# Gate rows spread by TensorE, a transposed first attention output, and high/low sums in place of f32 for one chunk

## What is computed

```python
x = x + 0.5 * _L0_ffn_ref(ln(x))    # MOE0_A: 16 experts 128->256->128, gelu, top 2
x = x + _L0_attn_ref(ln(x))         # ATT0: elu+1 features, sums over the sequence
x = x + 0.5 * _L0_ffn_ref(ln(x))    # MOE0_B
x = x + 0.5 * _L1_ffn_ref(ln(x))    # MOE1_A: 16 experts 128->128, relu, top 2
x = x + _L1_attn_ref(ln(x))         # ATT1: causal linear attention, 16 heads of 8
x = x + 0.5 * _L1_ffn_ref(ln(x))    # MOE1_B
```

## Time and profile before

| | |
|---|---|
| median of 3 runs | 703.26 us (699.38 to 709.02) |
| the profiled execution | 708.19 us, span 706.2 us |
| mean granted TensorE clock | 0.964 |
| TensorE busy | 655.9 us (93%) |
| VectorE, ScalarE, GpSimd busy | 465.5, 432.3, 181.3 us |

### The profile page before, as it was taken

How to read it: one execution, slowest core, us unless ns; L and a number is a source line. 1 busy time by engine, 2 the same in 40 slices (tenths; PEclk the granted TensorE clock), 3 DMA queues, 4 the chain that set the end, 5 groups by cost and what they waited for, 6 DMA issues and landing times.

```text
span 706.2 us, 7645 instructions
## 1 busy us (share of the span) xinstructions
PE 655.9 (93%) x2395; PEld 415.2 (59%) x2395; DVE 465.5 (66%) x1059; ACT 432.3 (61%) x922; POOL 181.3 (26%) x132
## 2 busy tenths in 40 slices
PE   3699998999999999999999999999999989889974
PEld 2456565556656555676576666666566645556552
DVE  5677467643447964737769957858886757386752
ACT  4345456444447554697486478657379524968685
POOL 3120000100002111144042025214014432676565
PEclk9899999999999999999999999989999998989998
DMA  8782621063333107612223222200613000000000
GB/s 244 162 164 67 112 63 38 22 122 65 102 75 60 59 3 132 96 26 65 42 61 62 65 55 60 60 1 11 111 60 61 0 1 0 1 15 1 16 16 15
DMA packets 27026, 42.22 MB, mean 60 GB/s; under 512 B 1689, under 2 KB 8938, under 8 KB 26986
## 3 DMA queue, kind: packets, MB, share of 16 engines
q1 hardware_dynamic: 26986, 41.74, 27.1%
HBM read 40.42 MB, written 1.31 MB: 59 GB/s over the span
## 4 chain that ended last, share of the span: by engine, by line
PE 67%; ACT 12%; DVE 9%; SPq 5%; DMA 4%; issue 2%; POOL 1%; POOLq 0%; ACTq 0%; DVEq 0%
PE py L1122 26%; PE ph L900 7%; PE ph L902 7%; PE ph L901 7%; ACT stage L547 5%; ACT bc L547 4%; DMA bc<-comb_rows 3%; PE ps L1030 2%; SPq L358 2%; DVE stage L756 2%; PE ps L1031 2%; PE ps L1032 2%; SPq L331 1%; PE ps L1004 1%; PE ps L1005 1%
## 5 line engine op out<-in xcount | busy, mean ns | idle before, releaser
L596 ACT ACTIVATE g<-ph,b1col 128x512 f32<-128x512 f32 x256 | 172.7, 695 | 153.3 <-PE ph L902 120.1
L1122 PE MATMUL py<-hw,w2s 128*128 128x512 f32 x512 | 250.0, 612 | 1.9 <-DVE hw L859 1.9
L859 DVE TENSOR_TENSOR hw<-g,bc 128x1024 f32<-128x1024 f32 x128 | 166.8, 1310 | 110.4 <-ACT g L596 93.2
L1122 PEld LDWEIGHTS py<-hw,w2s 128*128 128x128 f32 x512 | 97.2, 194 | 77.7 <-issue 64.4
L900 PE MATMUL ph<-xbh,w1h 128*128 128x512 f32 x256 | 137.4, 537 | 0.0
L388 POOL TENSOR_TENSOR rstd<-vare,mhalf 128x4 f32<-128x4 f32 x24 | 35.4, 1477 | 358.3 <-DVE vare L672 358.1
L547 ACT ACTIVATE stage<-ps,comb 128x128 f32<-128x128 f32 x384 | 106.3, 564 | 10.4 <-PE ps L1032 10.2
L902 PE MATMUL ph<-xbh,w1l 128*128 128x512 f32 x256 | 102.7, 401 | 0.0
L901 PE MATMUL ph<-xbl,w1h 128*128 128x512 f32 x256 | 102.6, 401 | 0.0
L448 POOL TENSOR_TENSOR stage<-stage 128x1024 f32<-128x1024 f32 x24 | 57.4, 2393 | 68.4 <-ACT stage L547 68.4
L900 PEld LDWEIGHTS ph<-xbh,w1h 128*128 128x128 f32 x256 | 49.7, 194 | 30.8 <-issue 22.6
(11 more groups left out here) (199 smaller groups left out, 865.0 us busy)
## 6 DMA issues: line engine op xcount, KB each, us to landing
bc<-comb_rows SPq DMA_DIRECT2D x31, 1024.0 KB, 8.8
stage<-in_L_ffn_W_dram SPq DMA_DIRECT2D x4, 512.0 KB, 6.5
X<-in_L_attn_x_dram SPq DMA_DIRECT2D x4, 256.0 KB, 3.1
bc<-comb_rows SPq DMA_DIRECT2D x4, 256.0 KB, 5.5
out_dram<-X SPq DMA_DIRECT2D x4, 256.0 KB, 2.3
comb_rows<-combT SPq DMA_DIRECT2D x8, 32.0 KB, 5.3
side<-in_L_attn_wq_dram SPq DMA_DIRECT2D x1, 64.0 KB
side<-in_L_attn_wk_dram SPq DMA_DIRECT2D x1, 64.0 KB
```

Of the source, the lines that this page charges most:

```text
L596: nc.scalar.activation(g[:, s % 2, h, 0:w], ph[:, (HC * s + h) % RING_PH, 0:w], ACT.Gelu, bias=b1col[:, HC * e + h:HC * e + h + 1]).then_i ...
L859: V.tensor_tensor(hw[:, s % RING_HW, :, 0:w], g[:, s % 2, :, 0:w], bc[:, s // GQ % 2, s % GQ, 0:w].unsqueeze(1).to_broadcast([P, HC, w]), ...
L1122: ins = T.matmul(py[:, 0:cols], w2s[:, w], hw[:, s2 % RING_HW, h, 0:cols], start=e2 == 0 and h == 0, stop=False)
```

## The change

Five edits and a new `TURNS` table.

1. The gate rows of the first three experts (`PE_GATES = 3`) are no longer read back from DRAM: TensorE spreads each over 128 partitions of `ps` by a matmul of a column of `ident` with `combT`, and VectorE reads them there. The fourth still comes by DMA.
2. ATT0's output is one matmul of `wos` by `vv` (128x512), so that it comes out transposed; the bias is added by the Gelu on ScalarE; four transposes on TensorE bring `osb` back, and VectorE adds from `ps`.
3. W2 and `expert_w` are loaded from ScalarE's DMA queue.
4. `EXACT_CUM` is (3, 4, 5): of the chunks that occur, 2 leaves it and 3 stays, so ATT1 of chunk 2 is summed from `kvh` and `kvl`.
5. The transpose of `expert_b` (start of `wt`) waits for three `hw` as well.

```diff
-    "ACT": ("l2 h l2 h2 l h9 m2 l3 m2 l2 m2 l m2 l3 m4 l2 m4 l m2 l4 m24 l3 m2 h m2 h m6 h m4 l2 m2 l m2 l5 m46 l3 m2 h m2 l2 h m6 "
+    "ACT": ("l2 h l2 h4 l m2 h7 m2 l3 m2 l2 m2 l m2 l5 m4 l m2 l4 m26 l3 m2 h2 m4 h m6 l2 m2 l m2 l5 m48 l3 m2 h m2 l2 h m4 h l m2 "
...
-    EXACT_CUM = (2, 3, 4, 5, 6, 7)
+    EXACT_CUM = (3, 4, 5, )
     LAG = 2
+    PE_GATES = 3
...
-            sp.dma_start(w2s[:, :].rearrange("p (e c o) -> p e c o", e=E, c=HC), W2.rearrange("e (c p) o -> p e c o", p=P)).then_inc(w_in["w2"], 16)
             sp.dma_start(b2s[:, :], b2).then_inc(w_in["w2"], 16)
...
-            sp.dma_start(bos[:, :], bo.rearrange("(a p) -> a p", a=1)).then_inc(w_in["small"], 16)
+            sp.dma_start(bqkv[:, 3:4], bo.rearrange("(p a) -> p a", a=1)).then_inc(w_in["small"], 16)
...
                     if k == 0:
-                        for e in range(GQ):
-                            sp.dma_start(bc[:, 0, e:e + 1, 0:wide(c)], comb_dram[l // 2, e:e + 1, col(c)].partition_broadcast(P)).then_inc(bc_first[e], 16)
+                        sp.dma_start(bc[:, 0, PE_GATES:GQ, 0:wide(c)], comb_dram[l // 2, PE_GATES:GQ, col(c)].partition_broadcast(P)).then_inc(bc_first, 16)
                         continue
...
                     if k == 1:
                         sp.wait_ge(w1_ready, W1_PARTS)
-                        sp.dma_start(stage[:, 0:E * D].rearrange("p (e h) -> p e h", e=E), expert_w.rearrange("e d h -> d e h")).then_inc(w_in["we"], 16)
...
                     nc.scalar.activation(w1h[:, w1_part(i)], stage[:, w1_part(i)], ACT.Copy).then_inc(w1_high, 1)
+                    if i == 0:
+                        act.dma_start(w2s[:, :].rearrange("p (e c o) -> p e c o", e=E, c=HC), W2.rearrange("e (c p) o -> p e c o", p=P)).then_inc(w_in["w2"], 16)
...
             def wt(l, c):
+                act.wait_ge(w1_ready, W1_PARTS)
+                act.dma_start(stage[:, 0:E * D].rearrange("p (e h) -> p e h", e=E), expert_w.rearrange("e d h -> d e h")).then_inc(w_in["we"], 16)
...
-                nc.scalar.activation(osb, ps[:, 1, :], ACT.Gelu_apprx_tanh).then_inc(a0["o"], 1)
+                nc.scalar.activation(osb, ps[:, 1, :], ACT.Gelu_apprx_tanh, bias=bqkv[:, 3:4]).then_inc(a0["o"], 1)
...
-                dve.wait_ge(a0["o"], c + 1)
-                V.tensor_tensor(X[:, col(c)], X[:, col(c)], osb, ALU.add).then_inc(a0["x"], 1)
+                dve.wait_ge(a0["ot_ps"], c + 1)
+                V.tensor_tensor(X[:, col(c)], ps[:, 2, :], X[:, col(c)], ALU.add).then_inc(a0["x"], 1)
...
-                    if s < GQ:
-                        dve.wait_ge(bc_first[s], 16)
+                    if s < PE_GATES:
+                        dve.wait_ge(gate_ps, s + 1)
+                    elif s == PE_GATES:
+                        dve.wait_ge(bc_first, 16)
...
+                    gates = ps[:, s, 0:w] if s < PE_GATES else bc[:, s // GQ % 2, s % GQ, 0:w]
+                    V.tensor_tensor(hw[:, s % RING_HW, :, 0:w], g[:, s % 2, :, 0:w], gates.unsqueeze(1).to_broadcast([P, HC, w]), ALU.mult).then_inc(hw_ready, 1)
...
             def q0(l, c):
+                l, c = MAIN[0]
+                pe.wait_ge(light["ct"], nth_light("ct", l, c))
+                for e in range(PE_GATES):
+                    T.matmul(ps[:, e, 0:wide(c)], ident[0:E, e:e + 1].to_broadcast([E, P]), combT[:, col(c)], start=True, stop=True).then_inc(gate_ps, 1)
                 yield
...
                 pe.wait_ge(a0["vz"], c + 1)
+                T.matmul(ps[:, 1, :], wos[:, :], vv, start=True, stop=True).then_inc(a0["o_ps"], 1)
+                yield
+                pe.wait_ge(a0["o"], c + 1)
                 for j in range(TPC):
-                    d = ps[:, 1, j * D:(j + 1) * D]
-                    T.matmul(d, vv[:, j * P:(j + 1) * P], wos[:, :], start=True, stop=False)
-                    ins = T.matmul(d, ones[0:1, :], bos[:, :], start=False, stop=True)
-                ins.then_inc(a0["o_ps"], 1)
+                    ins = T.transpose(ps[:, 2, j * P:(j + 1) * P], osb[:, j * P:(j + 1) * P], ident[:, :])
+                ins.then_inc(a0["ot_ps"], 1)
                 yield
...
             def wt(l, c):
                 pe.wait_ge(w_in["l1"], 16 * 6)
+                pe.wait_ge(hw_ready, PE_GATES)
```

10 lines of the change are left out of this document (4 added, 6 removed), and 32 rows, old and new, of the table TURNS.

## The result

The changed kernel takes 695.34 us (median of 20 runs, 693.29 to 700.25); before, run beside it, 706.21 us (20 runs, 699.38 to 710.43). The ratio is 0.9868, with a 95% interval of 0.9846 to 0.9889: 1.3% faster, where 2.2% was forecast. The profiled execution took 697.73 us with a span of 695.8; that of before 708.19 and 706.2.

A forecast was written before the change was run, and what follows sets the result against it. TensorE, busy 93% of the span, was taken to bound the kernel. Gains of 7 (start), 2 and 6.3 (ATT0's output, work and clock) and 0.4 (ATT1 of chunk 2) make 15.7 us off the median 703.26: 687.5 us, range 678 to 698.

The forecast's parts named there:

- ATT0's output: Four outputs of ATT0: 2 us gained in work, 6.3 us in clock, with two of four clock falls staying.
- The rival on the clock: At ATT0's outputs: the clock stays low at all four, since gaps remain and transposes are light; 694 us, chance 0.20.
- The start: Up to the eighth slot's `ph`: reached at 43.9 us instead of 50.66, 7 us gained, bounds 4 and 9.
- the first `hw` begins after the first gate and is done at about 23.5: At the start: first `hw` takes 1.22 us behind its gate matmul, so the first `py` starts near 24.4 us.
- The reason given for an earlier norm: At the start: X no longer stands behind the issue stall of 9.89 us; part of the 7 us gained.
- The tail: Behind the last bias row: 0.4 us gained by ATT1 of chunk 2 in parts, bounds -2 and 3.
- with the cheaper sums they do not run dry: Last chunk's ReLUs: the 2.35 us they ran dry before goes, so they reach 595.0 us instead of 595.39.
- The 2 us of later gates: In the tail: `kvl` and normaliser on VectorE put the last chunk's gates 2 us later, bounds 0 and 3.7.
- counted nothing: Tail from 595 us on: new order moves the ReLUs' gaps more than it removes them; 0, with 3 us either way.
- The prediction's own sign of being wrong: Forecast is wrong if the first `py` is later than 27 us, or the tail over 3 us longer or shorter.
- the sign of the forecast: ATT1 of chunk 2 summed in parts: a gain, of 0.4 us, bounds -2 and 3.
- the middle: From first to last bias row: 8.3 us gained, all at ATT0's outputs.

The follow-up runs named there:

- u_out: Changed kernel with ATT0's output as before, eight alternating f32 matmuls and no transposes, in the new order; ratio to before 1.0026.
- b_row_gates1: Kernel before with the bias as one wide row ahead of the wait, and three of the first four gates by TensorE; ratio to before 0.9754.
- u_queues: Changed kernel with the W2 and `expert_w` loads issued on SP again, at their old places; ratio to before 0.9896.
- a_group: Changed kernel with ATT0's output by the eight small matmuls grouped, four of one row, then four of 128 rows, behind the wait; ratio to before 0.9903.
- v_row: Changed kernel with ATT0's bias as one 512-column row ahead of the wait, then four 128x128 matmuls, no transposes; ratio to before 0.9879.
- v_tail: Changed kernel with the rest of the last chunk's routing on VectorE ahead of the normaliser and the third low part; ratio to before 0.9916.
- u_sums: Changed kernel with chunk 2's second attention back in f32 sums; ratio to before 0.9905.
- v_start: Changed kernel with the first `hw` ahead of chunk 1's `xn` and the first `py` ahead of its transposes; ratio to before 0.9875.
- v_xfirst: Changed kernel with chunk 1's X loaded ahead of `b2s` and the other small loads; ratio to before 0.9866.

## Why the prediction was right and wrong

**ATT0's output, right in kind and too small.** The forecast gave it 8.3 us (2 of work, 6.3 of clock). The changed kernel's trace shows 8.6 us of clock, since three falls went and one was halved, where I had kept two at 2 us each. With the small alternating matmuls the clock fell at 8 of 8 outputs (the kernel before and u_out); grouped, under the same wait, at none of 4, in one execution. The nine traces with the wide matmul show 5 falls at 36 outputs, and the six with one bias row ahead of the wait 4 at 24. Of these nine falls eight are at chunk 0, in 15 traces, where TensorE waits longest. So the alternating matmuls bring most of the falls, and idleness is left as a second cause, often at chunk 0 and rarely elsewhere. By u_out the whole edit is worth some 11 us.

The rival on the clock did not come: the granted clock was 1.00 in three stretches that hold the transposes and up to 2.2 us of idleness. The Trainium skill (TensorE: Matmul & The Clock Gate, Part 4: PE-mode transpose) says that transposes do not count as busy time of TensorE in the same way. No run here tests that: the four transposes take only 0.4 us at each output.

**The start, wrong: 7 us forecast, 1.6 measured at the eighth slot and 0.5 at the first bias row.** The step that failed is "the first `hw` begins after the first gate and is done at about 23.5". It was done at 26.89 us. The first gate was ready some 2.5 us before it began (its matmul starts at 22.27 us and takes 0.96); what it waited for was X of chunk 1, used at 21.95 us, and 3.7 us of VectorE's steps behind that. I had looked at the queue of TensorE there and not at VectorE's. The reading of before was wrong in the same way: the first `hw` at 28.60 us was put down to its gates' way through DRAM, but it waited for no DMA, and b_row_gates1 shows that quicker gates move it by nothing in the old order.

Two more errors stand behind this one. The reason given for an earlier norm, that X no longer stands behind the stall, brought 0.65 us in the trace (against u_queues). And I priced the first `py` at full clock, but the half clock came back from 25.0 to 31.7 us: 4.75 us of it behind the start of `py`, worth 2.4 us. With the 2.55 us by which `py` was late this makes 5.0 of the 5.2 us missing at the eighth slot. The profiled execution is also one of the later ones: u_out, a_group, v_row, v_tail and u_sums, with the same start, have their first bias row at 85.1 to 86.7 us, which is a gain of 0.7 to 2.3 us.

**The tail, wrong: 0.4 us gained was forecast, 3.5 us were lost.** The step that failed is "with the cheaper sums they do not run dry". The 2 us of later gates was right (21.2 against 19.1), but the ReLUs ran dry for 1.82 us. TensorE's timeline shows what held the `ph` that they waited for:

```profile
579.57 0.63 PE L1041 MATMUL ph<-weh,xbh 128*128 128x512 f32 x1
580.00 0.63 PE L1042 MATMUL ph<-weh,xbl 128*128 128x512 f32 x1
...
583.41 0.63 PE L1090 MATMUL ps<-kvh,ones_r 128*128 128x512 f32 x1
```

It waited 2.57 us for a low part (to 577.09 us), then ran at half clock until 584.5 us (`ph` matmuls 0.43 us apart instead of 0.23), and eight sums still stood ahead of the next `ph` (585.85 us). The half clock of before had come back, and nothing in the sum had a price for the new waits for low parts. The first 32 ReLUs end 32.25 us behind the row's start instead of 30.15. The other 1.4 us of the 3.5 are lost behind them, where I had counted nothing, with 3 us either way. The prediction's own sign of being wrong, a tail over 3 us longer, came true.

Whether the parts or the order make the tail long stays open. In the old order, the parts and ten moved steps together make it 139.1 us, beside 132.2 to 135.5 in the five traces without them, and cost 7.8 us in all. In the new order it is 137.4 to 141.0 us in the eleven traces with parts and 141.4 in the one without (u_sums), and taking the parts out gains nothing. There the sign of the forecast may even hold. Among the eleven, the tail is shortest where its mean granted clock is highest (137.4 to 137.7 us at 0.90) and longest where it is lowest (140.8 and 141.0 us at 0.86). Which of the two brings the other is not shown.

**The sum.** 15.7 us forecast in the trace, 10.4 measured: the start 6.5 short (by the first bias row), the middle 5.1 more, the tail 3.9 short. The measured 695.34 us lies in the range, near its upper end, and it does so by luck in part: the middle's surplus made up for half of what start and tail fell short. Of the middle's 13.4 us, 9.6 are the output (u_out); the other 3.8 come with the new order, and which of its moves bring them I did not test.

**What stays open.** Whether the first three gates by TensorE bring 1 us in the old order. What makes the tail of the new order long, and what part of it is half clock, which no edit here controls. The two start moves (v_start, v_xfirst) are under what this measurement can tell.

## What to carry to other kernels

Look for f32 matmuls of one row that alternate with those of 128 rows: one wide bias row, issued ahead of the wait, took 15 to 16 us of 705 off this kernel by itself, about half of it through the clock. When an instruction is released earlier, read what stands ahead of it on its own engine before counting the gain; and when work leaves the busiest engine in a stretch where that engine waits, count the chain that replaces it instead. A new edit is best tried on the old order with nothing else: a simpler form of one part of this change gave more than the whole.
